# Two layers of attention and feed-forward on one core: head outputs gathered dense from HBM, reciprocals of the softmax sums taken on 128x32, the output projection two pairs later

## The chip, the core and the metric

The program runs on one core of a Trainium2 chip. The core has five engines that run their own instruction lists side by side: TensorE (PE: matmuls, with its weight loads shown as PEld), VectorE (DVE), ScalarE (ACT), GpSimd (POOL) and SyncE (SP), which here only issues DMAs. Each waits on semaphores that others raise. Transfers are done by 16 DMA engines. The metric is the device time of one execution, in microseconds, smaller is better.

## The reference

Everything is float32; x and ctx are 64 sequences of 64 channels by 256 positions.

```python
x = x + xattn0(layernorm(x), ctx)      # 8 heads of 8 channels; q, k, v all from layernorm(x); band |q-k| <= 64
x = x + ffn0(layernorm(x))             # 256x256 weight, tanh/norm scaling of each row
x = x + xattn1(layernorm(x), ctx)      # q from x, k and v from ctx, rotary on q and k, no band
x = x + ffn1(layernorm(x))             # 256 -> 1024 -> 256, relu, 4-bit weights plus low-rank part

# the end of xattn0, per sequence
o = softmax(q @ k.T / sqrt(8)) @ v     # per head
o = o @ w_out.T + b_out                # "out"
y = relu(o.T) * ctx
r = w_ct.T @ y + b_ct                  # "mix"
# the end of xattn1
r = Wo @ o + bo                        # "out"
```

## The kernel before

The 64 sequences are taken as 32 pairs: two sequences of 64 channels fill the 128 partitions. A pair has 16 heads (HPP). Both attention layers run the same software pipeline over pairs, with rings of three buffers: an iteration `r` is 16 head steps `h`, and in it each engine works on several pairs at once. `at(r, k)` is the pair k places later (`p1`, `p2`, `p3` are 1, 2 and 3 later, `m1` one earlier). After a ramp the loop body holds three iterations; the few last ones are written out, and the last steps of the last pair are spread over the following feed-forward stage by the dictionaries called `tail`.

In iteration r TensorE, at step h, scores head h of pair p1 (`score_head`, L429, into one of three score banks, after a band matmul L427 in layer 0), VectorE takes the row maxima of those scores (`maximum`, L1044), TensorE scores head h of pair r again with keys and queries exchanged and the maximum subtracted (`shifted_head`, L445), ScalarE takes the exponent (L692), in layer 0 GpSimd masks it (L1250), and every fourth step TensorE multiplies four heads by the values (`values_group`, L468). The values carry a column of ones, so a 32-row block of the result holds the 8 channels of a head, then the sum of its exponents, then unused rows. The maxima go from columns to rows: they are split in three bf16 parts (`split_max`, L945 to L951), turned by TensorE (`turn_max`, L499, at h = 12 for heads 0 to 7 of p1 and at h = 3 for heads 8 to 15 of r), copied by ScalarE (L746) and carried by a DMA into the rows of Qs (`shift_rows`, L371).

Queries and keys of three bf16 parts each are laid out and copied by DMAs from SyncE's one list, in order: `load_side` (L330), `lay_out` of pair r+2 (L346, L349, three DMAs each; it waits until the shifted scores of pair r-1 are done), `shift_rows` of r, `replicate` of pair r+2 (L360 twice, then L362, Ks<-Ks, after waits for the lay-outs' landing), `shift_rows` of p1. The scores of pair r+2 start in the next iteration.

Behind the values ScalarE copies a half pair of head outputs from PSUM to `heads_sb` (`heads_out`, L738). TensorE turns it in four fp32 transposes (`turn_heads`, L510, at h = 14 for half 0 and at h = 5 of the next iteration for half 1). VectorE takes the reciprocals of the 16 sums (L1074) and multiplies (L1077, `normalise`) into `normed`. TensorE turns that back in two transposes (`turn_back`, L521, h = 8), ScalarE copies it (L752, `back_out`) and TensorE projects it (`project`, L479, h = 10). In layer 0 there follow a relu on ScalarE (L759), the product with ctx on GpSimd (`gate`, L1267) and a second projection, "mix" (h = 14). VectorE adds the result to X and takes the statistics for the next norm (`update`, L1090, L956).

PSUM banks A and B serve many small jobs; the table `JOBS` sets the order in which they take turns, and the semaphore values are computed from it.

## Time and profile before

| | |
|---|---|
| median of 3 runs | 1414.41 us (1407.34 to 1414.45) |
| the profiled execution | 1412.66 us, its span 1410.90 us |
| mean granted TensorE clock | 0.962 |
| busy, share of the span | PE 92%, PEld 63%, DVE 67%, ACT 62%, POOL 51% |
| the chain that ended last | PE 60%, POOL 12%, issue 11%, DVE 8% |
| DMA | 113.32 MB, mean 80 GB/s |

The page cuts the span in 40 slices of 35 us; a digit is the busy share in tenths. Layer 0's attention fills slices 1 to 16, the first feed-forward stage 17 and 18, layer 1's attention 19 to 33, the last feed-forward stage the rest:

```profile
PE   4888999999999988773799999999999989999998
DVE  5866878888778887368788888888888862111110
DMA  8455444444444441003344444444444310000000
```

Matmuls are pipelined, so a busy PE says that there was always one under way. An engine that is idle off the chain costs nothing.

### The profile page before, as it was taken

To read this page: it belongs to the slowest core of one execution; us is meant where nothing else is said; L and a number is where in the kernel's file an instruction comes from. 1 tells how busy PE (TensorE), PEld (TensorE's weight loads), DVE (VectorE), ACT (ScalarE), POOL (GpSimd) and SP (SyncE) were. 2 spreads that over 40 slices of the span, in tenths; PEclk is the share of its full clock that TensorE was granted. 3 is DMA by queue.
4 is the path that set the end of the run, shared out by engine and by line. 5 is a ranking of instruction groups with operands and counts; after the bars stand their busy time and mean duration, and the time that the engine had idled before them with its cause. 6 is when DMAs were issued, how large, how long until landed. Compare 5 with 4: busy or idle time off the path is not lost.

```text
span 1410.9 us, 37590 instructions
## 1 busy us (share of the span) xinstructions
PE 1291.8 (92%) x11228; PEld 889.4 (63%) x11228; DVE 952.0 (67%) x2163; ACT 874.6 (62%) x1910; POOL 712.6 (51%) x1297
## 2 busy tenths in 40 slices
PE   4888999999999988773799999999999989999998
PEld 2566777777777765562466666666666655766675
DVE  5866878888778887368788888888888862111110
ACT  2555666766666666462688888888888874122211
POOL 4466777777777786305456556556556511010000
PEclk8899999999999999895799999999999999999999
DMA  8455444444444441003344444444444310000000
GB/s 200 107 147 138 96 94 104 98 91 95 98 102 92 94 96 39 12 0 72 70 103 103 98 102 104 96 101 106 94 100 109 88 40 1 16 30 15 15 15 30
DMA packets 90803, 113.32 MB, mean 80 GB/s; under 512 B 13779, under 2 KB 82131, under 8 KB 83059
## 3 DMA queue, kind: packets, MB, share of 16 engines
q1 hardware_dynamic: 86912, 107.05, 33.2%
q10 hardware_dynamic: 3830, 5.49, 1.3%
q8 instruction: 34, 0.56, 0.2%
q14 instruction: 27, 0.22, 0.1%
HBM read 18.66 MB, written 4.19 MB: 16 GB/s over the span
## 4 chain that ended last, share of the span: by engine, by line
PE 60%; POOL 12%; issue 11%; DVE 8%; DMA 3%; ACT 2%; POOLq 1%; SPq 1%; DVEq 1%; ACTq 0%
PE bank L468 10%; PE bank L429 9%; PE bank L656 8%; PE bank L647 8%; PE bank L445 8%; PE bank L427 5%; PE bank L479 4%; DVE row_max L1044 3%; PE bank L510 3%; POOL rot L1232 2%; PE bank L618 2%; POOL Qp L1221 2%; PE bank L499 1%; POOL k_rest L1237 1%; POOL q_rest L1237 1%
## 5 line engine op out<-in xcount | busy, mean ns | idle before, releaser
L1044 DVE TENSOR_REDUCE row_max<-bank 128x2 f32<-128x384 f32 (+1 forms) x1024 | 599.7, 617 | 131.0 <-PE bank L429 128.9
L692 ACT ACTIVATE probs<-bank 128x384 f32<-128x384 f32 (+1 forms) x1024 | 534.3, 542 | 174.0 <-PE bank L445 167.4
L445 PE MATMUL bank<-Qs,Ks 128*128 128x192 bf16 (+1 forms) x2048 | 369.4, 262 | 23.6 <-ACT probs L692 16.3
L429 PE MATMUL bank<-Ks,Qs 96*128 96x192 bf16 (+1 forms) x2048 | 373.9, 265 | 13.3 <-DMA Ks<-Ks 8.5
L1250 POOL TENSOR_SCALAR_AFFINE_SELECT probs<-probs 128x256 f32<-128x256 f32 (+1 forms) x512 | 260.8, 533 | 147.2 <-ACT probs L692 128.5
L429 PEld LDWEIGHTS bank<-Ks,Qs 96*128 96x128 bf16 x2048 | 190.2, 99 | 124.2 <-issue 40.3
L468 PE MATMUL bank<-probs,V 128*32 128x192 f32 (+1 forms) x4096 | 251.6, 364 | 5.9 <-POOL probs L1250 4.6
L445 PEld LDWEIGHTS bank<-Qs,Ks 128*128 128x128 bf16 x2048 | 190.0, 98 | 51.1 <-ACT probs L692 27.8
L427 PE MATMUL bank<-band,ident 128*128 128x384 bf16 x512 | 170.6, 333 | 8.5 <-DMA Ks<-Ks 7.5
L468 PEld LDWEIGHTS bank<-probs,V 128*32 128x32 f32 x4096 | 108.5, 110 | 86.3 <-issue 46.0
L1187 DVE TENSOR_TENSOR X<-bank,X 128x256 f32 (+1 forms) x32 | 13.6, 424 | 185.6 <-PE bank L656 185.6
L1232 POOL TENSOR_TENSOR rot<-rot,rope 128x256 f32<-128x256 f32 x64 | 46.8, 731 | 130.3 <-ACT rot L721 130.3
L647 PE MATMUL bank<-Ks,up_w 128*128 128x512 f32 x256 | 111.8, 592 | 0.0
L1321 POOL TENSOR_TENSOR X<-X,down_b 128x256 f32 x32 | 23.1, 749 | 169.4 <-DVE xn L1019 169.4
L738 ACT ACTIVATE heads_sb<-bank 128x512 f32<-128x512 f32 x128 | 75.6, 591 | 29.3 <-PE bank L468 29.2
L647 PEld LDWEIGHTS bank<-Ks,up_w 128*128 128x128 f32 x256 | 48.4, 190 | 56.8 <-issue 56.4
L479 PE MATMUL bank<-xn,att_w 128*128 128x256 f32 x192 | 66.7, 434 | 15.4 <-DVE xn L1019 15.4
L510 PE MATMUL bank<-ident,heads_sb 128*128 128x128 f32 x512 | 78.7, 277 | 1.6 <-ACT heads_sb L738 1.6
L912 ACT ACTIVATE probs<-bank,up_b 128x512 f32<-128x512 f32 x32 | 22.0, 687 | 85.8 <-PE bank L647 85.8
L721 ACT ACTIVATE rot<-bank,att_b 64x256 f32<-64x256 f32 x128 | 60.0, 469 | 15.8 <-PE bank L479 12.7
L912 ACT ACTIVATE Qs<-bank,up_b 128x512 f32<-128x512 f32 x32 | 22.0, 687 | 76.1 <-PE bank L647 76.1
L1221 POOL TENSOR_SCALAR Qp<-q_rest 128x256 bf16<-128x256 f32 x64 | 54.4, 850 | 27.1 <-DVE q_rest L1054 21.7
(125 smaller groups left out, 1704.1 us busy)
## 6 DMA issues: line engine op xcount, KB each, us to landing
Ks<-Ks SPq DMA_DIRECT2D x64, 576.0 KB
Qs<-Qs SPq DMA_DIRECT2D x128, 192.0 KB
Qs<-Qp SPq DMA_DIRECT2D x192, 64.0 KB
Ks<-Kp SPq DMA_DIRECT2D x192, 64.0 KB
side<-in_ctx SPq DMA_DIRECT2D x64, 128.0 KB, 2.0
X<-in_x SPq DMA_DIRECT2D x4, 1024.0 KB, 13.9
out<-X SPq DMA_DIRECT2D x8, 512.0 KB, 2.9
Qs<-max_rows SPq DMA_DIRECT2D x128, 12.0 KB
```

The costliest lines, as they stand in the source:

```text
L427: nc.tensor.matmul(dst[:, 0:2 * win], ident16[:, :], band16[:, :], start=True, stop=False)
L429: last = nc.tensor.matmul(dst[:, blk * win:(blk + 1) * win], Qs[0:SHIFT_ROW, pair[1], h, blk * P:(blk + 1) * P], Ks[0:SHIFT_ROW, pair[1], ...
L445: last = nc.tensor.matmul(dst[:, blk * win:(blk + 1) * win], Ks[:, pair[1], h, blk * P:(blk + 1) * P], Qs[:, pair[1], h, start(blk):start( ...
L468: last = nc.tensor.matmul(dst[32 * j:32 * j + 32, first:first + win], V[:, pair[1], blk, head, :], probs[:, head % 8, blk * win:(blk + 1) ...
L479: nc.tensor.matmul(job_bank[b][:, 0:T], w[:, weight, :], source, start=True, stop=True).then_inc(s[f"{b}_filled"], 1)
L510: last = nc.tensor.transpose(job_bank["A"][:, (blk * 2 + g) * P:(blk * 2 + g + 1) * P], heads_sb[:, half, g * T + blk * P:g * T + (blk + 1 ...
L647: last = nc.tensor.matmul(bank[2 + hb % 2][:, :], up_w[:, blk, hb * P:(hb + 1) * P], xT[:, cu, blk, :], start=(blk == 0), stop=(blk == 1))
L656: last = nc.tensor.matmul(bank[4 + j % 2][:, 0:T], hidden[cu][:, hb, j * P:(j + 1) * P], down_w[:, hb, :], start=(hb == 0), stop=(hb == HB ...
L692: nc.scalar.activation(probs[:, h % 8, 0:2 * win], exp_bank[h % 2][:, 0:2 * win], ACT.Exp, scale=SCALE).then_inc(s["exped"], 1)
L1044: nc.vector.tensor_reduce(row_max[:, pair[1], h, :], bank_of(pair, h)[:, 0:2 * win].rearrange("p (b k) -> p b k", b=2), AX.X, ALU.max).the ...
L1221: nc.gpsimd.tensor_scalar(parts[:, u, 1, :], rest[:, u, :], 1.0, None, ALU.mult).then_inc(s[mid], 1)
L1250: return nc.gpsimd.affine_select(out=part, in_=part, compare_op=ALU.is_ge, fill=0.0, base=base, pattern=[[0, 4], [-sign, width]], channel_ ...
```

## The change

The transposes of the head outputs, the copy after them and the reciprocals on 128x16 are gone. In their place SyncE issues five DMAs for each pair, on tensors in HBM (`spill`, `inverse_dram`):

- `spill_heads`: heads_sb, both halves, to HBM, after the row of maxima of pair r and ahead of `replicate`.
- `gather_heads`, behind `replicate`: the sums come back as 128x32 (`sums`), the 8 rows of each head as a dense 128x256 (`normed`).
- `inverse_out`, of the pair before that, ahead of `lay_out`: the reciprocals go to HBM.
- `inverse_in`, ahead of `spill_heads`: they are read back, each row for 8 partitions, as 128x256 (`inverse`).

VectorE takes the reciprocals of pair r-1 at h = 13 (`invert`) and multiplies pair r-2 by them at h = 10 (`normalise`). TensorE projects pair r-2 at h = 13 and mixes pair r-3 at h = 10 in layer 0; relu, gate and update move with them. ScalarE's copy to `heads_sb` waits for the landing of the store before it instead of a transpose. The first feed-forward stage writes out 16 of its steps instead of 8, to hold the longer tails.

```diff
 JOBS = {
-    "A": [("q", AHEAD), ("heads1", -1), ("v", 2), ("max0", 1), ("heads0", 0)],
-    "B": [("max1", 0), ("k", AHEAD), ("back", -1), ("out", -1), ("mix", -1)],
+    "A": [("q", AHEAD), ("v", 2), ("max0", 1)],
+    "B": [("max1", 0), ("k", AHEAD), ("mix", -3), ("out", -2)],
 }
...
+            def spill_heads(pair):
...
+                wait_apart(e, (s["heads_out"], num(pair) * 2 + 2), (s["sums_in"], num(pair) * 16),
+                           (s["heads_in"], num(pair) * 16))
+                e.dma_start(bass.AP(spilled, 0, [[T, P], [P * T, 4], [1, T]]),
+                            heads_sb[:, :, :].rearrange("p a (b t) -> p (a b) t", t=T)).then_inc(s["spilled"], 16)
+            def gather_heads(pair):
...
+                wait_apart(e, (s["spilled"], (num(pair) + 1) * 16), (s["rcp_out"], num(pair) * 16))
+                e.dma_start(sums[:, :], bass.AP(spilled, HD * T, [[32 * T, HPP], [32, HD], [1, 32]])
+                            ).then_inc(s["sums_in"], 16)
+                wait_apart(e, job_wait(s, l, "B", "out", at(pair, -RING), "filled"))
+                e.dma_start(normed[:, pair[1], :], bass.AP(spilled, 0, [[32 * T, HPP], [T, HD], [1, T]])
+                            ).then_inc(s["heads_in"], 16)
+            def inverse_out(pair):
...
+                wait_apart(e, (s["rcp_done"], num(pair) + 1), (s["rcp_in"], num(pair) * 16))
+                e.dma_start(bass.AP(inverted, 0, [[32, P], [1, 32]]), sums[:, :]).then_inc(s["rcp_out"], 16)
+            def inverse_in(pair):
...
+                wait_apart(e, (s["rcp_out"], (num(pair) + 1) * 16), (s["normed"], num(pair)))
+                e.dma_start(inverse[:, :], bass.AP(inverted, 0, [[T, HPP], [0, HD], [1, T]])
+                            ).then_inc(s["rcp_in"], 16)
             def iteration(r):
-                load_side(at(r, AHEAD + 1 if l else 0))
+                load_side(at(r, AHEAD + 1 if l else -1))
+                inverse_out(at(r, -2))
                 lay_out(at(r, 2))
                 shift_rows(r, 1)
+                inverse_in(at(r, -2))
+                spill_heads(at(r, -1))
                 replicate(at(r, 2))
+                gather_heads(at(r, -1))
                 shift_rows(at(r, 1), 0)
...
-            tail = {0: lambda: values_group(TAIL, 3), 2: lambda: turn_heads(TAIL, 1), 4: lambda: turn_back(TAIL),
-                    5: lambda: project("B", "out", TAIL, WO, mixed_in[:, :],
-                                       lambda: wait_job(e, s, l, "B", "back", TAIL, "read"))}
+            else:
+                tail = {0: lambda: values_group(TAIL, 3), 1: lambda: project_out(TAIL2),
+                        7: lambda: project_out(TAIL)}
...
-                wait_job(e, s, l, "A", f"heads{half}", at(pair, -1), "filled")
+                wait_some(e, s["spilled"], num(pair) * 16)
                 nc.scalar.activation(heads_sb[:, half, :], pv_bank[:, :],
...
+            def invert(pair):
...
+                e.wait_ge(s["sums_in"], (num(pair) + 1) * 16)
+                nc.vector.reciprocal(sums[:, :], sums[:, :]).then_inc(s["rcp_done"], 1)
+            def normalise(pair):
...
+                heads = normed[:, pair[1], :]
+                wait_apart(e, (s["heads_in"], (num(pair) + 1) * 16), (s["rcp_in"], (num(pair) + 1) * 16))
+                nc.vector.tensor_tensor(heads, heads, inverse[:, :], ALU.mult).then_inc(s["normed"], 1)
...
                 for h in range(HPP):
-                    if h == 5:
-                        normalise(m1, 1)
                     if h == 6:
                         apply(at(r, AHEAD + 1))
-                    if h == (14, 10)[l]:
-                        update(m1)
-                    if h == 14:
-                        normalise(r, 0)
+                    if h == 10:
+                        normalise(at(r, -2))
+                    if h == (11, 15)[l]:
+                        update(at(r, (-3, -2)[l]))
+                    if h == 13:
+                        invert(m1)
                     maximum(p1, h)
```

SyncE's list in the loop of layer 0, one iteration, before:

```order
L330 DMA side<-in_ctx 128x256
L306 REGISTER_ALU
L306 ISA
L346 DMA Qs<-Qp 8x16x256 x3
L349 DMA Ks<-Kp 8x16x256 x3
L288 ISA
L371 DMA Qs<-max_rows 3x16x128
L358 ISA
L360 DMA Qs<-Qs 24x4096 x2
L362 DMA Ks<-Ks 72x1x4096
L288 REGISTER_ALU
L371 DMA Qs<-max_rows 3x16x128
```

and in the changed kernel:

```order
L330 DMA side<-in_ctx 128x256
L401 DMA inverse_dram<-sums 128x32
...
L346 DMA Qs<-Qp 8x16x256 x3
L349 DMA Ks<-Kp 8x16x256 x3
...
L371 DMA Qs<-max_rows 3x16x128
L408 DMA inverse<-inverse_dram 128x1x256
...
L382 DMA spill<-heads_sb 128x4x256
...
L360 DMA Qs<-Qs 24x4096 x2
L362 DMA Ks<-Ks 72x1x4096
...
L390 DMA sums<-spill 128x1x32
...
L393 DMA normed<-spill 128x1x256
...
L371 DMA Qs<-max_rows 3x16x128
```

One DMA now stands between the load of side and the lay-out, two between the first row of maxima and the copies, two between the copies and the second row of maxima. Layer 1's list has the same order.

VectorE's list around head steps 12 to 15 of an iteration of layer 1, before (L1044 is the maximum of one head; L1074 and L1077 are the old reciprocal and product):

```order
L1044 TENSOR_REDUCE row_max<-bank 128x2
L1043 REGISTER_ALU
L1044 TENSOR_REDUCE row_max<-bank 128x2
L288 REGISTER_ALU
L1074 RECIPROCAL rcp<-bank 128x16
L1075 ISA
L288 REGISTER_ALU
L1077 TENSOR_TENSOR normed<-bank,rcp 128x2x64
L1043 REGISTER_ALU
L1044 TENSOR_REDUCE row_max<-bank 128x2
```

and in the changed kernel, steps 10 to 14 (L1061 is the maximum, L1098 the new product, L1090 the new reciprocal with its wait L1089):

```order
L1098 TENSOR_TENSOR normed<-normed,inverse 128x256
L1060 REGISTER_ALU
L1061 TENSOR_REDUCE row_max<-bank 128x2
L1060 REGISTER_ALU
L1061 TENSOR_REDUCE row_max<-bank 128x2
L1060 REGISTER_ALU
L1061 TENSOR_REDUCE row_max<-bank 128x2
L1089 ISA
L1090 RECIPROCAL sums<-sums 128x32
L1060 REGISTER_ALU
L1061 TENSOR_REDUCE row_max<-bank 128x2
```

The reciprocal that stood before the maximum of head 14 and read a transpose now stands before that of head 13 and reads what a DMA brought.

## Rows read from the trace of the kernel before

**Rows 1.** Windows inside the loops: us, each engine's busy time, clock, DMA share, GB/s.

```profile
250.00:370.00 120.00, 116.81 (x1265) 86.07 (x1265) 96.20 (x248) 82.31 (x189) 87.07 (x159) 1.00 0.41 94
870.00:990.00 120.00, 117.64 (x1189) 78.68 (x1189) 103.97 (x199) 102.59 (x222) 71.86 (x142) 1.00 0.45 102
```

**Rows 2.** Timeline of SyncE, layer 0: start us, us, engine, line, operation.

```profile
300.78 2.02 SPq L346 DMA_DIRECT2D Qs<-Qp  x3
...
316.67 2.01 SPq L346 DMA_DIRECT2D Qs<-Qp  x3
```

**Rows 3.** Timeline of SyncE, layer 1.

```profile
914.02 2.02 SPq L346 DMA_DIRECT2D Qs<-Qp  x3
...
929.24 2.01 SPq L346 DMA_DIRECT2D Qs<-Qp  x3
931.30 1.93 SPq L349 DMA_DIRECT2D Ks<-Kp  x3
933.37 0.76 SPq L371 DMA_DIRECT2D Qs<-max_rows  x1
934.27 1.56 SPq L360 DMA_DIRECT2D Qs<-Qs  x2
936.48 0.82 SPq L362 DMA_DIRECT2D Ks<-Ks  x1
```

**Rows 4.** Windows of one microsecond, layer 1.

```profile
938.00:939.00 1.00, 1.00 (x11) 0.59 (x13) 1.00 (x3) 1.00 (x4) 0.92 (x2) 1.00 0.72 197
...
941.00:942.00 1.00, 1.00 (x11) 0.91 (x10) 0.68 (x2) 0.81 (x3) 0.81 (x2) 1.00 0.47 98
```

**Rows 5.** Timeline of TensorE, layer 1.

```profile
921.11 0.38 PE L521 MATMUL bank<-ident,normed 128*128 128x128 f32 x2
921.33 0.61 PE L488 MATMUL bank<-att_w,side 128*128 128x128 f32 x4
...
926.56 0.60 PE L510 MATMUL bank<-ident,heads_sb 128*128 128x128 f32 x4
927.00 0.38 PE L429 MATMUL bank<-Ks,Qs 96*128 96x256 bf16 x2
```

**Rows 6.** Timeline of ScalarE, layer 1 and its end.

```profile
937.07 0.39 ACT L752 ACTIVATE mixed_in<-bank 128x256 f32<-128x256 f32 x1
...
1179.07 0.59 ACT L738 ACTIVATE heads_sb<-bank 128x512 f32<-128x512 f32 x1
```

**Rows 7.** Timeline of VectorE, layer 1.

```profile
942.52 0.25 DVE L1074 RECIPROCAL rcp<-bank 128x16 f32<-128x16 f32 x1
942.89 0.29 DVE L1077 TENSOR_TENSOR normed<-bank,rcp 128x128 f32<-128x128 f32 x1
```

**Rows 8.** Windows with one load of side, and with one store of the result.

```profile
928.00:929.00 1.00, 1.00 (x17) 0.54 (x10) 0.60 (x2) 0.23 (x1) 0.00 (x0) 1.00 0.47 131
...
1206.00:1211.00 5.00, 5.00 (x14) 2.32 (x14) 2.61 (x5) 1.37 (x2) 2.90 (x4) 1.00 0.32 105
```

**Rows 9.** DMA issues of the page: KB each, median us to landing.

```profile
out<-X SPq DMA_DIRECT2D x8, 512.0 KB, 2.9
```

**Rows 10.** Line L330, load of side: issue ns min/median/max, then its landing.

```profile
L330 SPq DMA_DIRECT2D side<-in_ctx x64: 334/350/522, 43.1 to 1094.5; - x64
...
DMA to landing us min/median/max: 1.9/2.0/5.7
```

**Rows 11.** Chain of waits in order of time: start us, us, what.

```profile
86.32 8.44 DMA Qs<-max_rows
...
656.96 6.10 DMA Ks<-Ks
...
928.96 0.70 DVE row_max L1044
```

**Rows 12.** Timeline of VectorE after the loop of layer 1.

```profile
1186.44 0.48 DVE L1090 SCALAR_TENSOR_TENSOR X<-bank,out_bias,X 128x256 f32<-128x256 f32 x1 [5.22 <-PE bank L479]
```

**Rows 13.** Timeline of TensorE there.

```profile
1191.39 0.60 PE L636 MATMUL bank<-ident,xn 128*128 128x128 f32 x4
```

More of the change, by code:

```diff
@@ L136, in build @@
         heads_sb = sb("heads_sb", [P, 2, 2 * T])
-        rcp = sb("rcp", [P, 2, HPP])
-        normed = sb("normed", [P, RING, 2, P])
-        mixed_in = sb("mixed_in", [P, T])
+        normed = sb("normed", [P, RING, T])
+        sums = sb("sums", [P, 32])
+        inverse = sb("inverse", [P, T])
+        spill = nc.dram_tensor("spill", (4, P, T), fp32)
+        inverse_dram = nc.dram_tensor("inverse_dram", (HPP, T), fp32)
         relu_out = rot[:, 0, :]
@@ L255, in ff0_steps @@
         def ff0_steps(e, step, tail, norm=None):
-            for n in range(2 * FF0_RING):
+            for n in range(4 * FF0_RING):
                 if n in tail:
@@ L261, in ff0_steps @@
                 step((n // FF0_RING, n % FF0_RING))
[L262 to L264 removed]
+            with e.Fori(4, PAIRS // FF0_RING - 1) as i:
                 for u in range(FF0_RING):
@@ L500, in turn_max, with project_out @@
                                     ident16[:, :]).then_inc(s[f"{b}_filled"], 1)
-            def turn_heads(pair, half):
+            def project_out(pair):
                 if not active(pair):
                     return
-                wait_bank(e, s, l, "A", f"heads{half}", pair)
-                e.wait_ge(s["heads_out"], num(pair) * 2 + half + 1)
-                for blk in range(2):
-                    for g in range(2):
-                        last = nc.tensor.transpose(job_bank["A"][:, (blk * 2 + g) * P:(blk * 2 + g + 1) * P],
-                                                   heads_sb[:, half, g * T + blk * P:g * T + (blk + 1) * P],
-                                                   ident[:, :])
-                last.then_inc(s["A_filled"], 1)
@@ L515, in turn_back, with mix @@
-            def turn_back(pair):
+                project("B", "out", pair, WO, normed[:, pair[1], :],
+                        lambda: e.wait_ge(s["normed"], num(pair) + 1))
+            def mix(pair):
                 if not active(pair):
                     return
-                wait_bank(e, s, l, "B", "back", pair)
-                wait_job(e, s, l, "A", "heads1", pair, "read")
-                for blk in range(2):
-                    last = nc.tensor.transpose(job_bank["B"][:, blk * P:(blk + 1) * P],
-                                               normed[:, pair[1], blk, :], ident[:, :])
-                last.then_inc(s["B_filled"], 1)
@@ L542, in iteration @@
                                 lambda: l and e.wait_ge(s[f"side_in{p3[1]}"], (p3[0] + 1) * 16))
-                    if h == 5:
-                        turn_heads(m1, 1)
-                    if h == 8:
-                        turn_back(m1)
                     if h == 8:
                         project_v(p2)
-                    if h == 10:
-                        project("B", "out", m1, WO, mixed_in[:, :],
-                                lambda: wait_job(e, s, l, "B", "back", m1, "read"))
+                    if h == 10 and l == 0:
+                        mix(at(r, -3))
                     if h == 12:
                         turn_max("A", p1, 0)
-                    if h == 14 and l == 0:
-                        project("B", "mix", m1, 4, gated,
-                                lambda: e.wait_ge(s["gated"], num(m1) + 1))
-                    if h == 14:
-                        turn_heads(r, 0)
+                    if h == 13:
+                        project_out(m2)
                     score_head(p1, h)
@@ L746, in max_out @@
                 nc.scalar.activation(max_rows[:, half, :], max_bank[bk], ACT.Copy).then_inc(s[f"{bk}_read"], 1)
-            def back_out(pair):
-                if not active(pair):
-                    return
-                wait_job(e, s, l, "B", "back", pair, "filled")
-                nc.scalar.activation(mixed_in[:, :], job_bank["B"][:, 0:T], ACT.Copy).then_inc(s["B_read"], 1)
             def relu(pair):
@@ L788, in iteration @@
                         values_out(p2)
-                    if h == 10 and l == 0:
-                        relu(m1)
+                    if h == 14 and l == 0:
+                        relu(at(r, -2))
                     if h == 12:
```

72 lines of the change are left out of this document (39 added, 33 removed).

## The prediction

> **What bounds the kernel now.** I read the windows by stage first: in the loops of both attention layers TensorE is busy 117 us of every 120, at a granted clock of 1.00 (2.4 GHz), VectorE 80 to 87% [rows 1]. Next came the DMA issues of SyncE, because there an iteration begins with the lay-out of a pair: the same issue returns after 15.89 us in layer 0 (300.78 to 316.67) [rows 2] and after 15.22 us in layer 1 (914.02 to 929.24) [rows 3]. The issues of one iteration show a second cycle beside TensorE's. From the first lay-out (my zero, 929.24) SyncE issues without a long gap: lay-outs to +3.99, a row of maxima to +4.9, two copies Qs<-Qs from +5.03 to +6.6, the copy Ks<-Ks at +7.24 [rows 3]. In windows of one microsecond the DMA engines work on that copy at a share of 0.72 and 197 GB/s, and still at 0.47 in 941 to 942 [rows 4]: its data end near +12.7. TensorE needs the copied pair at the start of the next iteration, +15.2. So the transfers have 2.5 us to spare, less the landing, and TensorE's work decides.
>
> **What TensorE, ScalarE and VectorE lose.** Per pair two groups of four transposes and one of two leave TensorE. They cost the distance to the next start, not their mean duration: 926.56 to 927.00 is 0.44 us, twice, and 921.11 to 921.33 is 0.22 us [rows 5]. That is 1.1 us a pair; with nothing in its place the periods would be 14.8 and 14.1 us. ScalarE loses one copy of 0.39 us a pair [rows 6]. VectorE loses two reciprocals of 0.25 us and two products of 0.29 us [rows 7] and gets one reciprocal of 128x32 and one product of 128x256. The trace shows neither; each is of twice the elements, so I bound them by the old durations and their doubles, 0.25 to 0.5 and 0.29 to 0.58 us. VectorE's sum hardly changes (1.1 out, 0.5 to 1.1 in; I take 0.8). The second projection is as many matmuls as before; two pairs later costs only at the ends.
>
> **What SyncE and the DMA engines get.** Five DMAs a pair: the store of 128x4x256 (512 KB), the gathers of 128x32 (16 KB) and 128x256 (128 KB), the store of the reciprocals (16 KB) and their replicated read (128 KB). For the large store the nearest rows are the result's own stores of the same shape: 0.32 of 5 us of all engines, 1.6 us [rows 8], and 2.9 us from issue to landing [rows 9]. For 128 KB it is the load of side: 0.47 us of all engines [rows 8], 2.0 us to landing [rows 10]. For the 16 KB DMAs I take 0.3 us of data each, between nothing and that 0.47. An issue costs between 0.35 us (the load of side) [rows 10] and 0.76 us (the row of maxima) [rows 3]; I take 0.4 for the read, 0.65 for the large store, 0.6 for the store of the reciprocals.
>
> Where they stand matters more than their sum. The read of the inverse and the large store stand ahead of the copies Qs<-Qs. The gathers stand behind Ks<-Ks. VectorE's reciprocal waits for the gathered sums ahead of its maximum of head 13. And the store of the reciprocals waits for VectorE and stands ahead of the next lay-out. That closes a cycle the kernel did not have: lay-out, copies, gather of the sums, reciprocal, store of the reciprocals, next lay-out. While VectorE waits in it, the maxima of heads 13 to 15 are queued behind, and TensorE, with three score banks, stops at the next pair's first score. While SyncE waits, its whole list does.
>
> Its length, from the lay-out. The two issues put the copies back by 1.05 us, so the issues of Qs<-Qs end at +7.6; Ks<-Ks follows at +7.7 instead of +7.24, since SyncE waited 0.65 us ahead of it for landed lay-outs (935.83 to 936.48). In the DMA engines 1.6 + 0.5 = 2.1 us of data now lie ahead of the copies. The same gap takes 0.7 of it and I pass on 1.4: the data of Ks<-Ks end at 12.7 + 1.4 = +14.1. The sums' 0.3 us follow, +14.4. From last data to landing I count 1.2 us, the 2.0 us of side's load less 0.35 of issue and 0.47 of data: +15.6. Reciprocal 0.3 (near the shorter bound, since the small ones of 16 columns are mostly fixed cost, my guess), two hand-overs of 0.1 (my estimate from the gaps between dependent rows, 934.13 to 934.27 the longest here), issue 0.6: the next lay-out begins at **+16.7**, in both layers, since their lists are the same. Bounds: if all added data and issues are covered, the sums land with Ks<-Ks, whose landing took 6.1 us from its issue where a wait measured it [rows 11]: 7.24 + 6.1 = 13.3, and with 0.3 + 0.2 + 0.35 + 0.1 the cycle is 14.3, TensorE's own time. If all 2.1 us come through, the landing takes 2.0 us and the issue 0.76, it is 18.5.
>
> **Does the gather wait behind the copy?** In the ramp a 12 KB row of maxima landed 8.44 us after its issue, with the lay-outs' data ahead of it [rows 11], and the slowest load of side took 5.7 us instead of 2.0 [rows 10]. So small DMAs do queue.
> The Trainium skill, page "DMA: Bandwidth & Descriptors", section "Two DMAs through the same engine are not ordered", says that within one queue of one engine descriptors start in order. By that rule the sums wait for the copy and the cycle is the one just summed; were they let past it, it would be the all-covered one. The two rows speak for the rule, though in the ramp ScalarE's large loads ran beside.
> The same page, section "Why a DMA increments its semaphore by 16 and not by 1", would put a copy of 24 source and 72 target rows on 12 of 16 engines. The share of 0.72 agrees, and the gather, spread over all 16, still ends with its last engine.
>
> **The ends.** A lay-out and a gather both stand in 29 iterations of a layer. The other three of each only lose their transposes: 6 x 1.1 = 6.6 us. After layer 1 the last pair goes through store 2.9, gather 2.0, reciprocal 0.3, store 2.0, read 2.0, product 0.4 and projection 0.5, some 10 us after its last copy of heads ended at 1179.66 [rows 6], so its update starts near 1190.2 instead of 1186.44 [rows 12]. Four norms stand behind it, and TensorE turned their chunk at 1191.39 [rows 13] with 1.9 us of room: +2 us.
>
> **Sum.** 29 x (16.7 - 15.89) = 23.5; 29 x (16.7 - 15.22) = 42.9; -6.6; +2: +61.8 us. The profiled execution took 1412.66 us (its span is 1410.90), 1.75 below the median of 1414.41, which is little here: 1412.66 + 61.8 = **1474 us**, slower by 4.3%.
>
> **Rivals.**
> *Full gain* (0.22 with its partial forms). The sums overtake or are covered; the cycle is 14.3 us and TensorE's 14.8 decides in layer 0: 29 x (1.1 + 0.9) = 58 off, 6.6 off, 2 on, 1350. Partly, with 15.2 us, 1388. For it: 2.5 us of room and a DMA share of only 0.45 [rows 1]. Against it: small DMAs that waited, and a store ahead of the copies.
> *Cancelling* (0.08). A cycle near 15.6 us: layer 0 gains what layer 1 loses, 1406 to 1420.
> *Forecast* (0.50). 16.2 to 17.3 us: 1445 to 1509.
> *Late maxima* (0.20), slower still. The last maximum of a pair ended at 929.66, +0.4 [rows 11]. Behind the stalled reciprocal three of them, 0.7 us each, end 2.4 us after the sums land, +1.3 of the next iteration. Their split, transpose and copy come after, and SyncE has that row of maxima ahead of the stores and copies, with no slack today (933.23 to 933.37 [rows 3]). That adds 0.5 to 1.2 us to the cycle, and decides once the maxima end later than about +0.8. At 17.5 us: 58 x 0.8 = 46 more, 1521.
>
> The last two are slower, cancelling is mostly no change, the first is faster: faster 0.23, within 0.5% (what a measurement of this kernel can tell from no change) 0.07, slower 0.70. The forecast's own range is 1445 to 1509. For 8 in 10 I go down to 1370, into the full gain, and up to 1550, a cycle of 18 us.
>
> **What would show it.** Right: the lay-out returns every 16 to 17.5 us in both loops, with TensorE busy under 92%; the idle time before VectorE's reciprocal of the sums is released by the DMA sums<-spill, 1 to 3 us each time; SyncE waits for VectorE ahead of inverse_dram<-sums; the data of Ks<-Ks end 1 to 2 us later; TensorE has a gap before a pair's first score. Wrong: VectorE does not wait at the reciprocal, and the periods are 14 to 15 us; or TensorE or VectorE stops elsewhere, at ScalarE's copy of heads (it now waits for the store's landing), or at the product (its inverse I expect near +8, for a use near +9).

## The result, and the profile after

The changed kernel took 1545.45 us (median of 4 runs, 1543.84 to 1548.49) beside 1414.0 us for the kernel before on the same chip: a ratio of 1.0945 (95% interval 1.0912 to 1.0977), slower by 131 us. The direction and layer 1's part were forecast, the size was not: 62 us were expected, so the measured loss is more than twice the forecast. The profiled execution took 1543.84 us.

From the page of the changed kernel (its span is 1542.1 us): busy time of the engines, granted clock by slices, the chain that ended last by engine, and one group of instructions (count, then busy time and mean ns, then idle time in front and what ended it):

```profile
PE 1274.8 (83%) x10588; PEld 825.3 (54%) x10588; DVE 936.2 (61%) x2035; ACT 859.7 (56%) x1846; POOL 719.4 (47%) x1297
PEclk9999999999999999988599999999999999999999
PE 38%; DMA 17%; POOL 13%; SPq 11%; issue 9%; DVE 8%; ACT 3%; POOLq 0%; DVEq 0%; ACTq 0%
L522 PE MATMUL bank<-rot,att_w 128*128 128x256 f32 x64 | 25.2, 479 | 87.0 <-POOL rot L1288 87.0
```

No engine is fuller than before; TensorE fell from 92% to 83%. Transfers and their issues make up 28% of the new chain, where the old one had 3% and 1%. The 87.0 us of TensorE in front of the "mix" (L522 reading `rot`) are new and stood in no step of the forecast.

The two windows that answer to [rows 1] (us, the busy time of PE, PEld, DVE, ACT and POOL, clock, DMA share, GB/s):

```profile
250.00:370.00 120.00, 95.85 (x948) 65.67 (x948) 78.27 (x190) 63.22 (x144) 72.41 (x129) 0.93 0.46 120
870.00:990.00 120.00, 102.05 (x994) 61.59 (x992) 91.25 (x167) 92.39 (x192) 64.41 (x126) 1.00 0.53 139
```

In layer 0 TensorE is busy 96 us of 120 instead of 117, and its clock is 0.93 of full instead of 1.00; in layer 1, 102 instead of 118.

**Layer 1, one iteration of SyncE** (start, us, what), answering to [rows 3]:

```profile
988.58 2.07 SPq L346 DMA_DIRECT2D Qs<-Qp  x3
990.70 1.93 SPq L349 DMA_DIRECT2D Ks<-Kp  x3
992.87 0.77 SPq L371 DMA_DIRECT2D Qs<-max_rows  x1
993.84 0.58 SPq L408 DMA_DIRECT2D inverse<-inverse_dram  x1
994.77 0.38 SPq L382 DMA_DIRECT2D spill<-heads_sb  x1
995.32 1.62 SPq L360 DMA_DIRECT2D Qs<-Qs  x2
996.99 1.05 SPq L362 DMA_DIRECT2D Ks<-Ks  x1
998.32 0.90 SPq L390 DMA_DIRECT2D sums<-spill  x1
999.55 2.27 SPq L393 DMA_DIRECT2D normed<-spill  x1
1001.94 0.80 SPq L371 DMA_DIRECT2D Qs<-max_rows  x1
1003.09 0.35 SPq L330 DMA_DIRECT2D side<-in_ctx  x1
1004.62 0.33 SPq L401 DMA_DIRECT2D inverse_dram<-sums  x1
1005.21 2.04 SPq L346 DMA_DIRECT2D Qs<-Qp  x3
```

From lay-out to lay-out it is 1005.21 - 988.58 = 16.63 us, where 16.7 was forecast. SyncE pauses from 1003.44 to 1004.62, until VectorE has the reciprocals. VectorE beside it, answering to [rows 7]; the bracket holds the idle time before the row and what ended it:

```profile
1004.09 0.35 DVE L1090 RECIPROCAL sums<-sums 128x32 f32<-128x32 f32 x1 [1.88 <-DMA sums<-spill]
```

The sums were issued at +9.7 and VectorE's reciprocal could start on them at +15.5 (1004.09 - 988.58; forecast +15.6). Two views sum this up, the waits of the whole run (us in total, times, longest) and SyncE's own waits in 850 to 1200:

```profile
DVE sums L1090 <- DMA sums<-spill: 73.9, 35, 4.7
```

```profile
SPq L308 <- DVE sums L1090: 21.2, 21, 2.5
```

The chain of the changed kernel in that stretch shows a second way round, by the maxima behind the reciprocal:

```profile
1006.49 0.66 DVE row_max L1061
...
1009.13 0.28 ACT max_rows L770
1009.42 0.77 SPq L371
...
1015.00 5.78 DMA sums<-spill
```

VectorE's maximum at 1006.49 is the last of the three behind the reciprocal; as a row it goes out at 1009.42, and the last issue of the lay-out that started at 1005.21 ends near 1009.2. The two cycles, by the lay-out and by the late maxima, are tied to within a quarter of a microsecond, and the chain takes the one by the maxima.

**Layer 0, where the rest went.** GpSimd and TensorE around one mix of the changed kernel:

```profile
311.89 0.72 POOL L1288 TENSOR_TENSOR rot<-rot,side 128x256 f32<-128x256 f32 x1
315.05 1.00 POOL L1271 TENSOR_SCALAR_AFFINE_SELECT probs<-probs 128x256 f32<-128x256 f32 x2 [2.44 <-ACT probs L716]
```

```profile
309.06 0.33 PE L488 MATMUL bank<-Qs,Ks 128*128 128x192 bf16 x2
312.67 0.70 PE L522 MATMUL bank<-rot,att_w 128*128 128x256 f32 x2 [3.27 <-POOL rot L1288]
```

The change moves the mix from h = 14 to h = 10 in TensorE's list, while the gate (L1288), which makes what the mix reads, keeps its place in GpSimd's, behind the masks and the splits of q and k. So TensorE stops for 3.27 us with the scores of heads 10 to 15 queued behind it, ScalarE and VectorE run dry, and GpSimd itself then waits 2.44 us for an exponent. Behind this stop the matmuls keep their pace, and the granted clock stays at 1.00 (windows of 313 to 317 and 317 to 320). Behind the next stop, which ended at 331.16, it is 0.50 in 332 to 334. The chain shows the same pair of score matmuls at either level, at 300 us (2.4 GHz) and behind that stop (1.2 GHz); such stretches make the 0.93 of the window:

```profile
300.43 0.18 PE bank L472 x2
...
332.39 0.32 PE bank L472 x2
```

The kernel before, at the same place:

```profile
312.99 0.73 POOL L1267 TENSOR_TENSOR rot<-rot,side 128x256 f32<-128x256 f32 x1
```

```profile
314.51 0.62 PE L479 MATMUL bank<-rot,att_w 128*128 128x256 f32 x2
```

There the gate ended 0.8 us before the mix came, and nobody waited.

A period is the time from one lay-out to the next, a mean over 18 or 19 iterations in the middle of the loop. The sums run from the third lay-out of a layer to its last (29 periods). Both are read on the profiled executions, in us:

| run | median us | ratio, 95% | period layer 0 | period layer 1 | sum 0 | sum 1 |
|---|---|---|---|---|---|---|
| before | 1414 | 1 | 15.89 | 15.22 | 480.4 | 451.3 |
| changed | 1545.45 | 1.0945 (1.0912 to 1.0977) | 19.67 | 16.73 | 569.6 | 489.8 |
| gate first | 1467.37 | 1.0394 (1.0368 to 1.0421) | 16.70 | 16.69 | 494.1 | 490.6 |
| three pairs later | 1413.12 | 1.0022 (1.001 to 1.0034) | 15.79 | 15.83 | 475.8 | 464.5 |

Of the 131.2 us between the two profiled executions layer 0 has 569.6 - 480.4 = 89.2, layer 1 has 489.8 - 451.3 = 38.5, and 3.5 are left for the ends.

### The profile page after: what moved, and what is told of

It reads as the page before. It is cut to its first block, busy times and chain, and to the rows that moved or that the text cites. A ratio compares the mean times of both kernels' runs of the same rounds, so it can differ in the third digit from the quotient of the medians.

```text
span 1542.1 us, 36464 instructions
## 1 busy us (share of the span) xinstructions
PE 1274.8 (83%) x10588; PEld 825.3 (54%) x10588; DVE 936.2 (61%) x2035; ACT 859.7 (56%) x1846; POOL 719.4 (47%) x1297
## 4 chain that ended last, share of the span: by engine, by line
PE 38%; DMA 17%; POOL 13%; SPq 11%; issue 9%; DVE 8%; ACT 3%; POOLq 0%; DVEq 0%; ACTq 0%
DMA sums<-spill 12%; PE bank L680 7%; POOL probs L1271 7%; PE bank L671 6%; PE bank L511 6%; PE bank L472 4%; PE bank L488 4%; PE bank L470 4%; PE bank L522 3%; DVE row_max L1061 3%; SPq L360 3%; DMA spill<-heads_sb 2%; POOL Qp L1242 2%; PE bank L642 2%; ACT probs L716 2%
## 5 line engine op out<-in xcount | busy, mean ns | idle before, releaser
L1061 DVE TENSOR_REDUCE row_max<-bank 128x2 f32<-128x384 f32 (+1 forms) x1024 | 598.5, 615 | 242.1 <-PE bank L472 235.1
L472 PE MATMUL bank<-Ks,Qs 96*128 96x192 bf16 (+1 forms) x2048 | 380.3, 269 | 51.6 <-DVE row_max L1061 42.8
L488 PE MATMUL bank<-Qs,Ks 128*128 128x192 bf16 (+1 forms) x2048 | 376.4, 267 | 25.6 <-ACT probs L716 16.5
L472 PEld LDWEIGHTS bank<-Ks,Qs 96*128 96x128 bf16 x2048 | 187.0, 101 | 189.6 <-DVE row_max L1061 58.6
L511 PE MATMUL bank<-probs,V 128*32 128x192 f32 (+1 forms) x4096 | 262.3, 377 | 5.7 <-POOL probs L1271 4.4
L470 PE MATMUL bank<-band,ident 128*128 128x384 bf16 x512 | 177.1, 346 | 9.6 <-DMA Ks<-Ks 6.8
L522 PE MATMUL bank<-rot,att_w 128*128 128x256 f32 x64 | 25.2, 479 | 87.0 <-POOL rot L1288 87.0
L962 POOL TENSOR_SCALAR max_parts<-row_max 128x16 bf16<-128x16 f32 x64 | 16.2, 253 | 155.1 <-DVE row_max L1061 155.1
L522 PE MATMUL bank<-xn,att_w 128*128 128x256 f32 x192 | 67.1, 436 | 15.4 <-DVE xn L1036 15.4
L770 ACT ACTIVATE max_rows<-bank 48x128 bf16<-48x128 bf16 x128 | 34.6, 270 | 65.2 <-PE bank L542 64.9
```

Source lines behind the costliest of these rows:

```text
L470: nc.tensor.matmul(dst[:, 0:2 * win], ident16[:, :], band16[:, :], start=True, stop=False)
L472: last = nc.tensor.matmul(dst[:, blk * win:(blk + 1) * win], Qs[0:SHIFT_ROW, pair[1], h, blk * P:(blk + 1) * P], Ks[0:SHIFT_ROW, pair[1], ...
L488: last = nc.tensor.matmul(dst[:, blk * win:(blk + 1) * win], Ks[:, pair[1], h, blk * P:(blk + 1) * P], Qs[:, pair[1], h, start(blk):start( ...
L511: last = nc.tensor.matmul(dst[32 * j:32 * j + 32, first:first + win], V[:, pair[1], blk, head, :], probs[:, head % 8, blk * win:(blk + 1) ...
L522: nc.tensor.matmul(job_bank[b][:, 0:T], w[:, weight, :], source, start=True, stop=True).then_inc(s[f"{b}_filled"], 1)
L1061: nc.vector.tensor_reduce(row_max[:, pair[1], h, :], bank_of(pair, h)[:, 0:2 * win].rearrange("p (b k) -> p b k", b=2), AX.X, ALU.max).the ...
```

## Experiments

The recorded expectations call a run by what it changes; "e1" and "gate first" are experiment 1, "the half-store run" is 6, "the run without the gather" is 7, "the sums apart" is 5. Each ratio is to the kernel before, timed beside that run (1410.0 to 1411.8 us).

**1. The gate first.** Only GpSimd's list in layer 0 is changed.

```diff
+                    gate(at(r, -3))
                     mask_group(m1, 3)
...
                 if l == 0:
-                    gate(at(r, -3))
```

> The changed kernel with one edit: in layer 0 GpSimd multiplies by ctx (gate of pair r-3) first in its iteration instead of behind the masks and splits. Theory G (TensorE's 3.3 us stop before the mix at h = 10 comes from where the gate stands in GpSimd's list): the stop is gone, layer 0's period falls from 19.5 us to the 16.7 us of the cycle through the sums, 29 x 2.8 = 80 us less, about 1465 us, TensorE's granted clock in layer 0 back at 1.00, and VectorE now waits 1 to 3 us for the sums in layer 0 too. Rival D (layer 0 is long for the transfers; the gate's wait only covers it): TensorE stops elsewhere, period 18 to 19.5 us, 1510 to 1545 us.

1467.37 us, 78 us less, as theory G had it. The period of layer 0 fell from 19.67 to 16.70, which is the cycle forecast for it; the clock came back to 1.00:

```profile
250.00:370.00 120.00, 105.98 (x1139) 74.41 (x1139) 84.35 (x220) 74.78 (x174) 85.76 (x153) 1.00 0.55 142
```

Its waits in 130 to 480 show what had been hidden under the mix: VectorE waits for the sums, and TensorE for the maxima behind that.

```profile
DVE sums L1090 <- DMA sums<-spill: 50.5, 21, 3.1
PE bank L470 <- DVE row_max L1061: 33.7, 21, 2.4
```

So two mechanisms lie over each other in layer 0: the stop at the mix (78 us, what the lower clock costs included) and, under it, the cycle through the sums. Runs 5 to 8 start from this version, runs 9 to 11 from run 8.

**2. Transposes doubled**, in the kernel before, to price what the change takes out.

```diff
-                for blk in range(2):
+                for blk in (0, 1, 0, 1):
                     last = nc.tensor.transpose(job_bank["B"][:, blk * P:(blk + 1) * P],
```

(and the same for the four transposes of each half.)

> The kernel before with its transposes of head outputs issued twice into the same places (8 more matmuls of 128x128 for the heads and 2 more for the turn back, per pair). Theory: TensorE decides both loops, and a transpose costs its distance to the next start, 0.11 us: 64 x 1.1 = 70 us more, about 1484 us, periods 17.0 and 16.3 us. Rival: a part is hidden by waits of TensorE, under 40 us more.

1466.12 us, ratio 1.0381 (1.0349 to 1.0413): 54 us more, between the 70 of the theory and the 40 of the rival. Layer 0's period rose by 1.10 us, to 16.99, as forecast; layer 1's by 0.77, to 15.99. There TensorE had waited for the split maxima, 0.29 us a pair (4.7 us, 16 times in 850 to 1100), and the added work filled that wait. What adding the transposes costs is only an estimate of what leaving them out can give.

**3. The store of the reciprocals behind the lay-out.**

```diff
-                inverse_out(at(r, -2))
                 lay_out(at(r, 2))
+                inverse_out(at(r, -2))
                 shift_rows(r, 1)
                 inverse_in(at(r, -2))
```

> The changed kernel with the store of the reciprocals moved behind the lay-out in SyncE's list, so that the lay-out no longer waits for VectorE. Theory C (the cycle through the sums sets layer 1's period): the lay-out starts with TensorE's last shifted head again while VectorE's wait stays; the read of the inverse now waits about 1 us for the store's landing. Layer 1's period falls from 16.6 to 15.3 to 15.9 us, 20 to 38 us less, 1507 to 1525 us; layer 0, held by the gate, moves little. Rival V (VectorE's wait for late sums alone decides, wherever the store stands): 1540 to 1550 us.

1587.14 us, ratio 1.1252 (1.121 to 1.1293): slower still, outside both expectations. Layer 1's period went to 18.05 us. SyncE's timeline there:

```profile
1009.81 0.33 SPq L401 DMA_DIRECT2D inverse_dram<-sums  x1
1010.81 0.77 SPq L371 DMA_DIRECT2D Qs<-max_rows  x1
1013.25 0.59 SPq L408 DMA_DIRECT2D inverse<-inverse_dram  x1
...
1016.38 0.90 SPq L362 DMA_DIRECT2D Ks<-Ks  x1
```

The read (L408) follows its own store (L401) closely and now waits for the landing that the lay-out used to cover. Ks<-Ks goes out at +10.8 (its lay-out began at 1005.59) instead of +8.4, and the sums behind it. Taking the wait ahead of the lay-out away doesn't open the cycle, since it closes through the late maxima as well: in 850 to 1200 SyncE waits 21.4 us for rows of maxima (17 times), and 15.8 us for the landing of the reciprocals' store (13 times), which the run added to the way. The two are not told apart.

**4. The sums gathered from ScalarE's queue** at h = 12 or 11.

```diff
                     if h == VALUES_AT[l] + 9:
+                        gather_sums(m1)
                         heads_out(r, 0)
```

> The changed kernel with the 16 KB gather of the sums issued by ScalarE, on its own queue, just ahead of its copy of the first half of heads, instead of by SyncE behind Ks<-Ks. Theory Q (in the one queue the gather waits for the data of Ks<-Ks): issue to landing falls from a median of 5.8 to 2 to 3 us, VectorE's wait for the sums in layer 1 goes from 2 us a pair to under 0.3, and layer 1's period from 16.6 to 14.5 to 15.3 us: 38 to 60 us less, 1485 to 1507 us. Layer 0 is unchanged (the gate). Rival S (the DMA engines are simply full, whatever the queue): landing stays near 5 us, layer 1 above 16 us, over 1525 us.

1568.41 us, ratio 1.1113 (1.1085 to 1.114). The gather in ScalarE's queue and VectorE's reciprocal behind it:

```profile
1000.61 0.53 ACTq L774 DMA_DIRECT2D sums<-spill  x1
```

```profile
1006.53 0.35 DVE L1096 RECIPROCAL sums<-sums 128x32 f32<-128x32 f32 x1 [2.42 <-DMA sums<-spill]
```

The rival's time came (over 1525 us, layer 1 above 16 us). The median landing did fall from 5.8 to 2.4 us, but the reason is when the gather goes out and not from whose queue. In layer 0 (200 to 480) ScalarE issues it 7.7 to 8.9 us behind Ks<-Ks, and the reciprocal starts 2.0 us after the issue. In layer 1 (860 to 1180) it goes out 1.3 to 2.0 us behind Ks<-Ks, and the reciprocal follows after 5.3 to 6.4 us; in the row above it is 1006.53 - 1000.61 = 5.9 us, with Ks<-Ks issued at 999.03. From SyncE's queue it was 5.5 to 6.5 us, at 1.2 to 1.5 us behind the same copy. Another issuing engine does not carry a small gather past a large copy here, and the queue theory fails as it was put. Why this run is slower than the changed kernel (periods near 20.2 and 17.1 us) is not settled. The Trainium skill, page "DMA: Bandwidth & Descriptors", section "Issuing engines are not separate DMA queues", says that transfers started by different engines end up on the same 16 DMA engines and interleave. This run agrees, with 5.3 to 6.4 us beside the other queue's copy and 2.0 us well behind it.

**5. The sums stored and gathered apart** (with the gate first): the four partitions of heads_sb that hold the sums, 16 KB in all, have their own store, and their gather stands ahead of Ks<-Ks. (The two new functions are not shown.)

```diff
                 inverse_in(at(r, -2))
+                store_sums(at(r, -1))
                 spill_heads(at(r, -1))
-                replicate(at(r, 2))
+                replicate(at(r, 2), at(r, -1))
```

> The kernel of e1 (gate first), with the rows of sums stored apart: a 16 KB store of 4 partitions of heads_sb to HBM ahead of the 512 KB store, and the gather of the sums from there ahead of Ks<-Ks. One more DMA a pair on SyncE. Theory C (both periods of e1, 16.6 and 16.8 us, are the cycle through sums that wait for Ks<-Ks): the sums land near +12.5 of the iteration instead of +15.5, VectorE waits under 1 us, and the periods fall to what the landing of Ks<-Ks and TensorE allow, 14.8 to 15.8 us: 58 x 0.9 to 1.9 less than 1467, 1357 to 1415 us. Rival T (the copies, pushed back by the store, are already as late as the sums): the sums come early but TensorE waits for Ks<-Ks instead, periods above 16.2 us, over 1440 us.

1436.89 us, ratio 1.020 (1.017 to 1.0229): 30 us less than with the gate alone, between the two expectations. Nearly all of it is in layer 0, whose period fell from 16.70 to 15.89; layer 1 stayed at 16.55 (16.69 before), as rival T had it. VectorE's wait for the sums is gone from both loops. But with the small store and the gather ahead of it, Ks<-Ks goes out at +9.8 in layer 0 and +10.4 in layer 1 (medians) instead of +8.3 and +8.4. So in the wait's place TensorE waits for the copy, in layer 0 at the first band matmul of a pair (130 to 480):

```profile
PE bank L487 <- DMA Ks<-Ks: 14.8, 22, 1.3
```

In layer 1 (850 to 1100) it waits 0.35 us a pair for the copy, 0.43 for a row of maxima and 0.97 for their split. So this run shows that the wait for the sums can be had away, and not what the cycle costs in layer 1.

**6. Half of the large store left out** (with the gate first; half 1 of the head outputs is not stored, so the gathers read old values there).

```diff
-                e.dma_start(bass.AP(spilled, 0, [[T, P], [P * T, 4], [1, T]]),
+                n = 4 if isinstance(pair[0], int) and num(pair) == 0 else 2
+                e.dma_start(bass.AP(spilled, 0, [[T, P], [P * T, n], [1, T]]),
```

> The kernel of e1 with half of the large store left out (blocks of the second half pair are stored for the first pair only; the output is that of stale data). It shows what the store's own data cost. Theory (the store's 1.6 us of all DMA engines lie ahead of the copies and pass into the cycle for the most part): 0.5 to 0.8 us less a pair, 58 x 0.65 = 38 us less, about 1430 us. Rival: the store's data fit into gaps and only the places of the issues count, under 10 us less, 1457 to 1467 us.

1435.41 us, ratio 1.0193 (1.0158 to 1.0227). 256 KB less ahead of the copies is worth 16.70 - 16.14 = 0.56 us in layer 0 and 16.69 - 16.11 = 0.58 in layer 1: the store's bytes do come through into the cycle, as the theory had it. A part of that lies in SyncE's list: the issue of the sums behind Ks<-Ks takes 0.61 us at the median instead of 0.98.

**7. The gather of the sums left out** (with the gate first; VectorE inverts a buffer that no transfer fills).

```diff
-                e.dma_start(sums[:, :], bass.AP(spilled, HD * T, [[32 * T, HPP], [32, HD], [1, 32]])
-                            ).then_inc(s["sums_in"], 16)
```

> The kernel of e1 with the gather of the sums left out: VectorE takes the reciprocal of a buffer that is never refilled, and waits for no DMA there (the output is not normalised by the right sums). It shows what everything but that cycle costs. Theory C: the periods are TensorE's 14.1 to 14.8 us, at most 15.2, 58 x 1.5 to 2.3 less than 1467, 1335 to 1380 us. Rival T (the copies are as late as the sums): over 1430 us, with TensorE waiting for Ks<-Ks.

1396.98 us, ratio 0.9913 (0.9883 to 0.9943): 70 us less than with the gate alone, and between the two expectations. Not all of it is the wait's, since an issue is gone from SyncE's list too, and the gather behind it is issued in 0.78 us at the median instead of 2.37. Run 8, which keeps every transfer, gets 54 us of the 70. The periods stop at 15.20 and 15.67 us, where the forecast's list of TensorE alone would be 14.8 and 14.1. TensorE hardly waits for the copy Ks<-Ks in layer 1 (850 to 1100: 1.1 us, 3 times), but in every pair for the split maxima:

```profile
PE bank L541 <- POOL max_parts L967: 15.3, 16, 1.0
```

That is 0.96 us a pair, against 0.29 in the kernel before. It leaves 15.67 - 14.1 - 0.67, some 0.9 us a pair of layer 1, that no wait of TensorE explains.

**8. Everything three pairs later** (with the gate first). The products come for the pair three places back, so that no wait is for a transfer just issued.

```diff
                 lay_out(at(r, 2))
                 shift_rows(r, 1)
+                inverse_out(at(r, -2))
                 spill_heads(at(r, -1))
                 replicate(at(r, 2))
+                inverse_in(at(r, -2))
                 gather_heads(at(r, -1))
...
+                    if h == 2:
+                        invert(at(r, -2))
+                    if h == 5:
+                        normalise(at(r, -3))
```

(the lines taken out are the old places of these four; projection, relu, gate, mix and update move by one pair.)

> The changed kernel with the gate first, and the whole chain through HBM spread over one more iteration: the gathered sums of pair r-1 are inverted by VectorE in the next iteration at h = 2 (no wait for a transfer just issued), their store stands on SyncE behind the first row of maxima, their read behind Ks<-Ks, the product comes at h = 5 for the pair three places back and the projection one pair later still. No transfer is left out. Theory C (the lay-out waited for the sums, so a chain that is never waited for costs only its bytes and issues): no wait of VectorE for DMA sums<-spill in either loop, periods between those of the run without the gather (15.20 and 15.67 us) and those with the sums apart (15.89 and 16.55): 15.4 and 15.9 us, which from the gate-first run's 16.70 and 16.69 (1467 us) is 29 x (1.30 + 0.79) = 61 off, some 4 more at the ends: about 1410 us, 1395 to 1425. Theory B (the bytes ahead of and beside Ks<-Ks set the period, and VectorE's wait only took up time that was lost anyway): TensorE waits for DMA Ks<-Ks or for the late maxima instead, periods stay above 16.2 us in layer 1, over 1430 us.

1413.12 us (12 runs) beside 1410.17, as theory C had it: ratio 1.0022 (1.001 to 1.0034), slower by 0.2% and no change by the bound of half a per cent. All of the work is done, and 54 us of the gate version's 1467 are gone. The wait for the sums is gone from both loops. In layer 0 (130 to 480) TensorE waits in every pair for the copies instead, 1.1 us together, which the kernel before does not:

```profile
PE bank L471 <- DMA Ks<-Ks: 16.1, 22, 1.3
PE bank L489 <- DMA Qs<-max_rows: 7.8, 22, 0.9
```

The longest of SyncE's own waits in 850 to 1100, of the kernel before and then of this one:

```profile
SPq L371 <- ACT max_rows L746: 68.7, 17, 4.2
SPq L308 <- PE bank L445: 20.2, 16, 1.4
```

```profile
SPq L309 <- PE bank L489: 1.7, 5, 0.3
SPq L372 <- ACT max_rows L772: 1.3, 6, 0.3
```

Before, SyncE waited 100 us of 250 for others; here it waits 3.6, so its list is full. One of its issues (ns min/median/max) is longer than any other:

```profile
L391 SPq DMA_DIRECT2D sums<-spill x64: 520/2202/2540, 72.2 to 1182.2; - x64
```

The issue of this 16 KB gather takes 2.2 us at the median, with Ks<-Ks and the read of the reciprocals issued just ahead of it. In the changed kernel its issue takes 0.94 us and that of the next one, L393, 2.37. In both it is the second issue behind Ks<-Ks that is long, whatever its size. So a part of the full list looks like waiting for transfers queued ahead, and this run doesn't tell a full list from full DMA engines.

**9. The large store cut in two**, from run 8: half 0 goes behind the gathers.

```diff
-                spill_heads(at(r, -1))
+                spill_half(at(r, -1), 1)
                 replicate(at(r, 2))
                 inverse_in(at(r, -2))
                 gather_heads(at(r, -1))
+                spill_half(r, 0)
```

> The version with the chain spread over one more iteration, and its 512 KB store cut in two of 256 KB: half 1 of pair r-1 stays ahead of the copies, half 0 of pair r goes behind the gathers (three places in HBM in turn, so that no store waits for a gather). All bytes are moved. Theory B (bytes ahead of Ks<-Ks set the period): half of the store less ahead of it is worth what leaving it out was worth in the half-store run, 0.56 us a pair: periods 15.2 us in both loops, 29 x 1.15 = 33 off 1413, 1380 us (1375 to 1392), faster than the kernel before. Theory T (with three pairs of distance it is ScalarE's and GpSimd's turn that TensorE waits for, and SyncE's number of issues): the periods stay at 15.6 to 15.9 us, and the time at 1405 to 1420 us.

1430.02 us, ratio 1.0129 (1.0108 to 1.015): slower than run 8, and outside both expectations. The bytes taken from ahead of Ks<-Ks now lie ahead of the second row of maxima. TensorE's wait for the copy falls from 16.1 to 5.0 us (130 to 480), and its wait for that row rises from 7.8 to 25.8:

```profile
PE bank L491 <- DMA Qs<-max_rows: 25.8, 22, 1.5
```

One more issue in a full list comes on top; its share was not measured apart.

**10 and 11. Issues moved to ScalarE**, from run 8: both gathers, and in run 11 the read of the reciprocals too.

```diff
+                    if h == VALUES_AT[l] + 10:
+                        gather_heads(m1)
                     exp_head(r, h)
```

> The version with the chain spread over one more iteration, with the two gathers issued by ScalarE (at h = 13 in layer 0, h = 12 in layer 1, behind its copy of half 0) instead of SyncE; all bytes are moved as before. Theory Q (SyncE's list is the bound: in 850 to 1075 us it spends 187 us of 225 on issues and waits only 3.6 us of 250 in all, where the kernel before spends 123 us and waits 100; the issues of the two gathers take 2.20 and 0.79 us at the median): SyncE gets 3 us of room a pair, ScalarE gets some 1 us of issue, the periods fall from 15.79 and 15.83 to 15.2 to 15.4 in layer 0 and 15.3 to 15.5 in layer 1, 1385 to 1400 us, faster than the kernel before. Theory B (bytes): nothing moved less, the periods stay within 0.15 us, 1405 to 1420 us. Theory A (ScalarE is too full in layer 1, 97 us of 120): its waits for the store's landing and its issues push the exponents back and the time goes above 1430 us.

> The same with the replicated read of the reciprocals issued by ScalarE as well, one head step later (SyncE's issue of it takes 1.06 us at the median). Theory Q: if SyncE still bounds the gathers' version, another 0.5 us a pair, 15 to 20 us less than that; if it no longer does, no change, or up to 15 us more for ScalarE's 0.5 us of issue a pair. Theory B: 1405 to 1420 us.

1453.48 us, ratio 1.0309 (1.0295 to 1.0324), and 1454.77, ratio 1.0314 (1.0295 to 1.0333): theory A's outcome. SyncE got its room: in 850 to 1150 it waits 77 us. TensorE's waits for the copy and for the row of maxima nearly vanish in layer 0 (0.4 and 0.5 us in 130 to 480), but it waits 25.7 us there for exponents. ScalarE's gathers and next exponents in run 10:

```profile
1023.93 0.53 ACTq L778 DMA_DIRECT2D sums<-spill  x1
1024.64 0.96 ACTq L781 DMA_DIRECT2D normed<-spill  x1
1025.77 1.68 ACT L717 ACTIVATE probs<-bank 128x512 f32<-128x512 f32 x3 [1.72 <-PE bank L488]
```

From 1023.93 to 1025.77 no exponent runs. (The releaser named is a matmul; the two issues of the engine itself fill that time, up to 1025.60.) TensorE, which needs an exponent before it can reuse a bank, stops with it, and the periods go to 16.57 and 16.52 us. The section of the Trainium skill named at run 4 calls the issuing time, which is all that another engine saves, usually small beside the transfer; here it was 0.53 and 0.96 us on ScalarE and about 3 us on SyncE, and it was not free for the engine that took it over. Whether GpSimd could issue them more cheaply was not tried. No version that does all of the work beat the kernel before.

## Why the prediction was right in direction and too small

- **Failed step: "The second projection is as many matmuls as before; two pairs later costs only at the ends."** The count is right, but the mix was moved by four head steps in TensorE's list, and its producer, the gate, by none in GpSimd's. That made a wait of 3.3 us a pair in layer 0 (87.0 us over the run) and took the clock to 0.93. Run 1 shows the price of both together: 78 us. The forecast for layer 0, 23.5 us, compares with 89.2 measured, and with 494.1 - 480.4 = 13.7 once the gate stands first (the steady iterations lose 0.81 us each, as summed; the three longest, which fill the pipeline, are together 58.8 us instead of 64.5). The prediction's own signs of being wrong included a stop elsewhere, but named ScalarE's copy and the product, not the mix.
- **Luck:** 1545 us lies inside the wider range, up to 1550. That end was priced as a cycle of 18 us, not as a stop at the mix.
- **The cycle through the sums was right.** Its length was forecast at 16.7 us and measured at 16.73 in layer 1, 16.70 in layer 0 under the mix; sums there at +15.5 (forecast +15.6), reciprocal 0.35 us (0.3), SyncE waiting for VectorE ahead of inverse_dram<-sums. Layer 1's term, 42.9 us, came out at 38.5. Run 7 opened the cycle and got 70 us back, an issue less included; run 8 took the wait away with all transfers kept and got 54.
- **Bytes of the store coming through to the copies: right in size.** I passed on 1.4 of 2.1 us for all transfers ahead; half of the large one is worth 0.56 to 0.58 us (run 6), so the whole one some 1.1 by estimate.
- **Small transfers behind large ones: right, the reason narrower than I had it.** The order within one queue was not what mattered: from another engine's queue the gather took 5.3 to 6.4 us beside the same copy, from the same queue 5.5 to 6.5 (run 4). So the order of starts in one queue, on which the prediction weighed that page of the Trainium skill, is neither shown nor refuted, and did not decide. The share of 0.72, read as agreeing with 12 of 16 engines, is that of one microsecond; the next one, 939 to 940, shows 0.91, so that reading is not borne out.
- **The late maxima, a rival at 0.20**, were there, but tied with the lay-out rather than above it: the chain goes through L371 at 1009.42. I had them decide once they end later than +0.8; here the last ended at +1.9 (1007.15 - 1005.21) and the row went out 0.2 us behind the lay-out. In run 3, where the lay-out no longer waited, the period rose to 18.05 us.
- **The full gain, a rival at 0.22 with 1350 us, was not there to be had.** Even with the gather left out, the time is 1397. I priced TensorE's list at 14.8 and 14.1 us with nothing in the way; in layer 1 the wait for the split of the maxima grew from 0.29 to 0.96 us a pair, and some 0.9 us a pair stays unexplained.
- **Not priced at all: SyncE's list.** I laid issues only on the way to Ks<-Ks. One iteration of the changed kernel holds 13.1 us of issues in 16.63 (the rows above), against 8.2 in 15.22 before (the issues of [rows 3], a second row of maxima and a load of side). It decides nothing while the cycle is 16.7 us, but it appears to be what keeps run 8 at 15.8: its waits are 3.6 us of 250. This is argued from that wait view, not shown by a run: the long issues may themselves be waits for full DMA engines, and runs 10 and 11 relieved SyncE but stopped ScalarE.
- **The ends** cost some 3.5 us, where -4.6 was forecast.

## What to carry to other kernels

When an operation moves in one engine's list, look up its producer and its consumer in the other engines' lists: one that stays behind makes a stop in every iteration, and that costs more than the work moved. A round trip through HBM is free only if nobody waits for it within the iteration; count the distance from issue to use against the landing of the largest copy queued near it (5.8 us here), not against what the transfer takes alone (1.9 us at the least). And count the issuing engine's list as a resource: five more DMAs a pair took its issues from 8.2 to 13.1 us an iteration, and moving them to a busy engine put their issue time into that engine's work.

## What the runs showed of the hardware that was not expected

- The issue of a small DMA can take four times its shortest time: 2.2 us at the median (0.52 at the least) for a 16 KB gather in run 8, 2.37 us (0.53) for the 128 KB one in the changed kernel. Both are the second issue behind a 576 KB copy; the first behind it takes 1.1 and 0.94 us.
- What a 16 KB gather takes goes by the copy it runs beside and not by the queue it is issued from: 5.3 to 6.4 us until its reader starts, at 1.3 to 2.0 us behind a 576 KB copy of another queue; 5.5 to 6.5 us behind the same copy in the same queue; 2.0 us at 7.7 to 8.9 us behind it.
- With stops of TensorE of 3.3 us in each period of 20 us the granted clock of the stretch is 0.93 instead of 1.00, a mean of stretches at 2.4 GHz and stretches at 1.2 GHz (0.50 in 332 to 334, behind one stop; 1.00 in 313 to 320, behind another). With the stops gone it is 1.00 again at 106 us busy of 120.
